# Value products of two units in one go, and a third buffer of probabilities

## The reference

```python
q, k, v = x @ Wq, c @ Wk, c @ Wv          # 16 heads of 8; c is x itself, or the context of 77 rows
s = softmax(q @ k.T / sqrt(8))            # per head, 128 x 128 or 128 x 77
x = x + (s @ v) @ Wo
# L0a is linear attention: phi(z) = elu(z) + 1, s = tril(phi(q) @ phi(k).T), rows divided by their sums
```

## Time and profile before

| | us |
|---|---|
| median of 3 runs | 5074.99 |
| lowest and highest | 5069.90, 5075.92 |
| the profiled execution, its own time | 5068.93 |
| its span, first to last instruction | 5067.10 |
| PE busy | 3738.8 |
| DVE busy | 3032.4 |
| ACT busy | 2023.0 |
| mean granted TensorE clock | 0.862 |

### The profile page before, as it was taken

How to read it: one execution, slowest core, us unless ns; L and a number is a source line. 1 busy time by engine, 2 the same in 40 slices (tenths; PEclk the granted TensorE clock), 3 DMA queues, 4 the chain that set the end, 5 groups by cost and what they waited for, 6 DMA issues and landing times.

```text
span 5067.1 us, 78547 instructions
## 1 busy us (share of the span) xinstructions
PE 3738.8 (74%) x26058; PEld 2373.0 (47%) x26058; DVE 3032.4 (60%) x7031; ACT 2023.0 (40%) x3182; POOL 923.4 (18%) x1314
## 2 busy tenths in 40 slices
PE   3858878766877797766786787876588688786655
PEld 1645545323664464533465545543356455453333
DVE  2434883776554586478455378467655558737834
ACT  1223445343333443534333344544334344453422
POOL 0000330331000123133001023133100012303300
PEclk6979999878888998987798899988799799897767
DMA  6020021222121003030321102122211200213121
GB/s 213 1 94 12 26 76 43 86 76 100 53 84 59 21 27 104 10 127 31 110 79 47 55 34 72 47 82 76 102 53 59 82 15 28 73 45 120 34 96 44
DMA packets 181704, 328.76 MB, mean 65 GB/s; under 512 B 13265, under 2 KB 122161, under 8 KB 180913
## 3 DMA queue, kind: packets, MB, share of 16 engines
q1 hardware_dynamic: 181296, 323.59, 18.7%
HBM read 231.87 MB, written 91.67 MB: 64 GB/s over the span
## 4 chain that ended last, share of the span: by engine, by line
issue 38%; PE 32%; DVE 12%; POOL 7%; DMA 5%; ACT 5%; SPq 2%; DVEq 0%; POOLq 0%; ACTq 0%
PE bank L1645 4%; POOL sb_big L1973 4%; PE bank L1656 3%; PE bank L1860 3%; PE bank L988 2%; PE bank L967 2%; POOL sb_rs L1413 2%; DVE sb_big L2075 2%; PE bank L492 2%; PE bank L547 2%; DMA sb_big<-key_parts 1%; DMA sb_big<-query_parts 1%; PE bank L915 1%; PE bank L970 1%; PE bank L946 1%
## 5 line engine op out<-in xcount | busy, mean ns | idle before, releaser
L1973 POOL TENSOR_TENSOR sb_big<-sb_big 128x512 f32<-128x512 f32 x384 | 496.6, 1299 | 862.3 <-PE bank L1860 534.2
L1860 PE MATMUL bank<-sb_big,sb_weights_const 128*128 128x512 f32 x768 | 482.0, 714 | 87.4 <-DVE sb_big L2080 85.6
L1936 ACT ACTIVATE bank<-sb_big,sb_Aneg 128x512 f32<-128x512 f32 x512 | 351.9, 687 | 422.5 <-DVE sb_big L2075 312.6
L2075 DVE TENSOR_TENSOR_SCAN sb_big<-bank,sb_big 128x512 f32<-128x512 f32 x384 | 467.4, 1217 | 82.8 <-ACT bank L1936 73.5
L1116 ACT ACTIVATE sb_big<-bank 77x512 f32<-77x512 f32 (+1 forms) x512 | 302.5, 592 | 454.0 <-PE bank L988 411.4
L967 PE MATMUL bank<-sb_big 128*77 128x128 bf16 (+1 forms) x2560 | 356.6, 230 | 164.5 <-issue 72.1
L1231 DVE TENSOR_REDUCE sb_small<-bank 128x4 f32<-128x308 f32 (+1 forms) x512 | 265.8, 525 | 318.9 <-PE bank L946 311.8
L1413 POOL TENSOR_TENSOR sb_rs<-sb_ve,sb_weights_const 128x4 f32<-128x4 f32 x112 | 113.6, 1015 | 1821.9 <-DVE sb_ve L1399 1821.9
L967 PEld LDWEIGHTS bank<-sb_big 128*77 128x77 bf16 (+1 forms) x2560 | 267.7, 115 | 261.8 <-issue 202.9
L970 PE MATMUL bank<-sb_topT,sb_pick 128*77 128x128 bf16 (+1 forms) x2048 | 298.9, 226 | 0.0
L1656 PE MATMUL bank<-sb_weights_L1f,sb_big 128*128 128x128 f32 x2048 | 280.6, 281 | 12.3 <-DVE sb_x L1725 11.7
(11 more groups left out here) (334 smaller groups left out, 7717.3 us busy)
## 6 DMA issues: line engine op xcount, KB each, us to landing
sb_big<-query_parts SPq DMA_DIRECT2D x160, 512.0 KB, 6.6
sb_big<-state_rows SPq DMA_DIRECT2D x128, 512.0 KB, 3.8
query_parts<-sb_big SPq DMA_DIRECT2D x120, 384.0 KB, 3.3
sb_big<-key_parts SPq DMA_DIRECT2D x64, 512.0 KB, 9.0
sb_big<-context_key_parts SPq DMA_DIRECT2D x64, 308.0 KB, 3.5
key_parts<-sb_big SPq DMA_DIRECT2D x48, 384.0 KB, 4.4
context_key_parts<-sb_big SPq DMA_DIRECT2D x48, 231.0 KB, 3.9
sb_big<-masked_key_parts SPq DMA_DIRECT2D x32, 308.0 KB, 3.8
```

The costliest lines, as they stand in the source:

```text
L1860: last = pe.matmul(m.bank[s][2 + half][:, :], m.const["ident"], M.h(s, 2 * (n % 2) + half), start=n == 0, stop=n == NS - 1)
L1936: act.activation(M.dA(s), M.dl(s, half), ACT.Exp, scale=m.Aneg[:, NS * half + n:NS * half + n + 1])\
L1973: pool.tensor_tensor(M.h(s, 2 * (n % 2) + half), M.b_rows(s, n // 2)[:, n % 2, :], M.du(s, half), ALU.mult)\
L2075: dve.tensor_tensor_scan(h, M.dA(s), h, 0.0, ALU.mult, ALU.add)\
```

## The change

A unit's value products are no longer written at its own tick. Those of an even unit are put off by one tick, and stand right ahead of those of the odd unit after it. So that its exponential needn't wait for products that are now issued later, there is a third buffer of probabilities, in `m.xT[s]`, and an exponential (or a causal product) waits for the value products of three units earlier.

```diff
-        if 0 <= tick - self.pv_lag < self.units:
-            out.append(("pv", tick - self.pv_lag))
+        pair = tick - self.pv_lag - 1
+        if pair % 2 == 0 and 0 <= pair < self.units:
+            out += [("pv", pair), ("pv", pair + 1)]
...
     def pT(self, s, u):
-        return cut(self.m.big[s], 8768 + 512 * (u % 2), 4, T)[0:self.Tk]
+        if u % 3 == 2:
+            return cut(self.m.xT[s], 0, 4, T)[0:self.Tk]
+        return cut(self.m.big[s], 8768 + 512 * (u % 3), 4, T)[0:self.Tk]
...
     def probabilities(u):
         act.wait_ge(*g.at("turn", (A.key, u)))
-        if u >= 2:
-            act.wait_ge(*g.at("pv", (A.key, u - 2)))
+        if u >= 3:
+            act.wait_ge(*g.at("pv", (A.key, u - 3)))
...
     def causal_products(u):
         dve.wait_ge(*g.at("turn", (A.key, u)))
-        if u >= 2:
-            dve.wait_ge(*g.at("pv", (A.key, u - 2)))
+        if u >= 3:
+            dve.wait_ge(*g.at("pv", (A.key, u - 3)))
```

## The result

The changed kernel takes 5006.61 us (median of 4 runs, 4994.65 to 5014.12), the kernel before in the same comparison 5072.49 (4 runs, 5069.9 to 5075.92). The ratio is 0.9868, with a 95% interval from 0.9846 to 0.9889: 66 us less. The time lies inside the wide range of 5003 to 5090, but outside the forecast's own range of 5030 to 5065, and the gain is more than twice the 27 us forecast. The profiled execution took 5005.06 us, with a span of 5003.1.

A forecast was written before the change was run, and what follows sets the result against it. PE was taken to bound some windows fully and share the bound in others. Joins 36 plus buffer 4 less waits 5 and 8 gave 27 us off 5068.9: 5042, median 5048; range 5030 to 5065, wide range 5003 to 5090.

The forecast's parts named there:

- Joins and their price: On PE, joining two units' value products saves 0.22 us; about 290 batches fewer save 64 us of PE.
- How much of it reaches the end: PE's saving of 1.6 us per sublayer counts fully in 13 sublayers, half in 19, not in 8: 36 us.
- For the alone ones and L1x beside L3f I count nothing: In these 8 sublayers PE waits for the scores' maximum; two ticks cost 2.29 against 2.22 us, so no gain.
- What the third buffer gives: On ACT, exponentials of even units start earlier, those of odd units gain nothing; 4 us taken.
- The bound of 71 us: Most ACT time the third buffer could free: 174 exponentials of even units, each up to 0.41 us earlier.
- Costs of 5 and 8 us: PE's added waits: 5 us between scores and shifted products, 8 us for the copy of bank 3 before turning back.
- All of PE's saving counts: Rival: every batch that goes is on the path, Mamba's windows included; 64 us gain, 5005 to 5015; chance 0.15.
- The saving turns into waits: Rival: PE reaches the next bank or copy sooner and waits there, nothing is left; 5075; chance 0.18.
- The late reader of the scores' bank: Rival: beside Mamba the scores' maximum comes late and the odd tick grows by 0.22; 22 us slower, 5097; chance 0.13.
- The granted clock: Rival: longer PE waits beside Mamba lower its clock from 1.00; about the time of before, 5076; chance 0.05.
- A join is worth less: Rival: a join saves PE only the 0.11 us of going in; 9 us gain, 5066; chance 0.06.

The follow-up runs named there:

- e3: The changed kernel with a one-column full-width product put between the two halves of each pair of value products: 5056.47 us, ratio 0.9962.
- e1: The kernel before with only the third buffer and its shorter waits, value products still one unit at a time: 5015.67 us, ratio 0.9879.
- e4: The changed kernel with the turning back of a group one tick later: 4991.74 us, ratio 0.9834.
- e9: The kernel before with four buffers of probabilities and no pairing: 5018.87 us, ratio 0.9898.

## Why the prediction was right in sign and short in size

**Joins and their price: right.** 303 batches were forecast, 303 stand there. 286 of them are a single pair, which takes 0.56 to the next start where PE doesn't wait behind it. A join is worth 0.22 us of PE by e3's timeline, and PE's saving with enough buffers was 61 us against 64.

**How much of it reaches the end: the first step that failed.** The shares were 13 sublayers in full, 19 half and 8 not at all, 36 of 64 us. With enough buffers 55 of 61 came through, nine tenths, and the table shows every kind of window gaining. (With the three buffers of the change pairs gave 9, for the reason of the next paragraph.) "For the alone ones and L1x beside L3f I count nothing" was the plainest miss: they gained 1.3 and 1.4 us each, though the steady pair does cost 2.29 against 2.22. That sum held for two ticks in the middle of a group and was carried over to a whole sublayer. L3a alone with four buffers takes 16.05 us from its first value products to its last turning back; one unit at a time it takes 18.56. With the first value products a tick later in pairs (1.11), 1.4 us remain, and they come at the groups' ends and in the tail without scores.

**What the third buffer gives: the step that failed most.** "An odd unit gains nothing: it now waits for the first half of the pair, which stands where its own wait ended before", and 4 us in all. The first half of the sentence is right, 256 us of such waits remain. The bound of 71 us was no bound: it gave an even unit 0.41 us, the length of a batch, where a wait took 411 / 348 = 1.18 on average, and the waits fell by 155. What was wrong above all is that such a wait is cheap. The reasons given were that ACT is 40% busy and that the freed bank isn't wanted before the pair is through. But an exponential that waits holds up what stands behind it on ACT, the copy of bank 3 and the partner's copies, however idle the engine is on average, and its own bank is wanted: PE's waits for the three fell by 19, 13 and 16 us in e1. Buffers alone gave 56 us, and running the pairs with three buffers instead of four cost 43. So what the third buffer gave depends on the order of counting: 60 us ahead of the pairs, or 13 if the pairs are given their full 55. Neither number could be read from the net result.

**Costs of 5 and 8 us: too high.** Shifted products and scores wait 2.6 us longer for maxima, not 5. The turning back does wait longer, 21 us in total, but the 22.8 us that value products waited for the same copy are gone. In waits for that copy this comes to nothing (49.1 and 47.3), where 8 was charged; e4 shows that 15 us could still be had around it with three buffers.

**The rivals.** "All of PE's saving counts" named 5005 to 5015, and the time is there by luck: it had no 56 us for buffers and no 43 us for the waits, which happened to cancel nearly. "The saving turns into waits" fell with L3a alone. The late reader of the scores' bank fell with the windows beside Mamba, which are all shorter. The granted clock of the window shown stayed at 1.00, and it was 0.860 over the whole span, 0.862 before. "A join is worth less" fell with e3.

In sum the forecast was 36 + 4 - 5 - 8. Measured by parts it is 55 for pairs, 56 for buffers and 43 lost to the third buffer's scarcity, with the copies and maxima inside these numbers. What stays open is how the 56 us of time divide between the copy of bank 3, the partners' copies and the banks that the exponentials free. The trace divides PE's waits (19, 13 and 16 us), but only the copy was moved by itself, with 9 to 12 net.

## What to carry to other kernels

A wait in an idle engine's queue is not free when two streams share the queue: price it by what stands behind the waiting instruction and who waits for that, and sum the bottleneck engine's waits for that engine over all lines. Where a change joins work into larger pieces, give it as many buffers as the piece and the lag need (here four for pairs), and time the buffers alone and the joining alone; here each is worth about 55 us, and with one buffer too few 43 of it was lost. A steady cycle that cancels says nothing of the ends of the groups.

## What the runs showed of the hardware

The price of changing tile shapes showed in one run apart from everything else: a full-width product of a single column between two narrow batches costs PE 0.22 us and the program 0.16; with a narrow one in its place the program pays 0.04. That fits the 0.11 in and 0.12 out read from the earlier trace rows.

A sublayer that runs alone can start at half the clock. Windows over the start of L3a alone, in the kernel before and in e1, from the first shifted products to the first value products (same columns as the windows above); the kernel before:

```profile
4934.60:4938.50 3.90, 3.90 (x34) 3.44 (x33) 2.07 (x3) 2.44 (x3) 0.88 (x4) 0.50 0.39 158
```

And in e1:

```profile
4896.90:4899.90 3.00, 2.88 (x38) 2.46 (x41) 2.00 (x3) 2.56 (x4) 0.63 (x3) 0.79 0.61 244
```

Before, the granted clock was 0.50 (1.2 of 2.4 GHz) over all 3.9 us; in e1 it returned within the 3.0 us (0.79 on average). In both, PE had stood some 17.6 us for a transfer ahead of this sublayer's scores, and the clock was 0.50 when they started; in the kernel before:

```profile
4929.60 1.98 PE L946 MATMUL bank<-sb_big 128*128 128x128 bf16 x16 [17.72 <-DMA sb_big<-key_parts]
```

 In e9, which has the same order of PE's work as e1, the first value products came 3.95 us after the first shifted ones, as in the kernel before (3.96), and not 2.98. So about 1 us of this sublayer's time, 0.24 us in the "alone" row's mean of four, is where the clock happens to return, and belongs to neither buffers nor pairs.
